# A mixture of experts in two groups of token tiles in place of three, and two small norm steps moved to GpSimd

## The reference, cut to what matters

```
t = _to_tokens(x)
t = t + _L0_ffn_ref(_ln_t(t), L0_ffn_Wg, L0_ffn_W1, L0_ffn_b1, L0_ffn_W2, L0_ffn_b2)
x = _from_tokens(t, x)
x = x + _L1_conv_ref(_ln_c(x), ...)
```

## Time and profile before

| | us |
|---|---|
| median of 3 runs | 867.4 |
| lowest and highest run | 866.68, 870.57 |
| the profiled execution | 865.79 |
| its span, first to last instruction | 864.0 |
| TensorE busy | 709.4 (82%) |
| VectorE busy | 559.6 (65%) |
| ScalarE busy | 353.9 (41%) |
| GpSimd busy | 276.7 (32%) |

### The profile page before, as it was taken

The page is one execution under the profiler, slowest core; times in us unless marked ns, Lnnn a source line. Parts: engine busy times, 40 slices in busy tenths (PEclk is TensorE's granted clock), DMA queues, the critical chain, the costliest instruction groups (busy, mean ns, idle before and its releaser), DMA issues.

```text
span 864.0 us, 13817 instructions
## 1 busy us (share of the span) xinstructions
PE 709.4 (82%) x4364; PEld 565.9 (66%) x4364; DVE 559.6 (65%) x2110; ACT 353.9 (41%) x889; POOL 276.7 (32%) x339
## 2 busy tenths in 40 slices
PE   6998988999779999979779985877875676686768
PEld 5886877988658999864368963555553443453336
DVE  7988742233342631477930225999999999989774
ACT  1000443554422223225412113887785664574322
POOL 5105162506440000024610022665555444533200
PEclk9999999999979999979979999999798999998989
DMA  8803255767500566600005100000000002001020
GB/s 345 295 1 98 79 163 149 205 184 217 214 14 26 195 219 241 246 1 0 1 1 201 56 1 0 1 2 1 2 1 1 1 4 47 2 13 50 13 50 25
DMA packets 27286, 72.64 MB, mean 84 GB/s; under 512 B 3000, under 2 KB 11576, under 8 KB 24528
## 3 DMA queue, kind: packets, MB, share of 16 engines
q1 hardware_dynamic: 25168, 67.56, 23.9%
q0 software_dynamic: 2048, 4.20, 1.6%
HBM read 61.61 MB, written 10.14 MB: 83 GB/s over the span
## 4 chain that ended last, share of the span: by engine, by line
PE 52%; DVE 31%; issue 6%; ACT 5%; POOL 5%; DMA 1%; SPq 0%; DVEq 0%; POOLq 0%; ACTq 0%
PE PB L1056 6%; PE PB L930 6%; PE PB L944 5%; PE PB L1272 5%; DVE arena L2633 3%; DVE top L2644 3%; PE PB L861 3%; DVE top L2628 3%; DVE arena L2647 3%; PE PB L851 2%; PE PB L1450 2%; DVE XT L1973 2%; PE PB L1034 2%; PE PB L1359 1%; PE PB L810 1%
## 5 line engine op out<-in xcount | busy, mean ns | idle before, releaser
L802 POOL TENSOR_TENSOR arena<-arena 128x512 f32<-128x512 f32 x64 | 81.3, 1270 | 120.9 <-ACT arena L1918 120.9
L1359 PE MATMUL PB<-ring 128*128 128x256 f32 x256 | 75.5, 422 | 17.7 <-ACT arena L1910 17.0
L1584 PE MATMUL PB<-w_first,arena 128*128 128x128 f32 x256 | 45.2, 304 | 52.6 <-POOL arena L802 52.0
L602 POOL TENSOR_TENSOR lnrs<-lnve,mhalf 128x4 f32<-128x4 f32 x20 | 20.5, 1026 | 210.1 <-DVE lnve L1956 206.0
L1634 ACT ACTIVATE arena<-PB,arena 128x128 f32<-128x128 f32 x212 | 60.2, 366 | 55.0 <-PE PB L930 55.0
L1584 PEld LDWEIGHTS PB<-w_first,arena 128*128 128x128 f32 x256 | 31.6, 153 | 77.7 <-POOL arena L802 72.7
L1918 ACT ACTIVATE arena<-arena,nmx 128x256 f32<-128x256 f32 x128 | 58.2, 506 | 58.8 <-DVE arena L2647 58.5
L930 PE MATMUL PB<-arena 128*128 128x128 f32 x424 | 60.2, 287 | 9.8 <-DVE arena L2172 5.3
L1359 PEld LDWEIGHTS PB<-ring 128*128 128x128 f32 x256 | 48.1, 209 | 29.6 <-issue 18.9
L930 PEld LDWEIGHTS PB<-arena 128*128 128x128 f32 x424 | 54.2, 201 | 12.9 <-issue 6.6
L944 PE MATMUL PB<-ring,arena 128*128 x424 | 59.5, 285 | 0.8 <-ACT arena L1634 0.7
(11 more groups left out here) (335 smaller groups left out, 1567.3 us busy)
## 6 DMA issues: line engine op xcount, KB each, us to landing
ring<-in_taps_dram SPq DMA_DIRECT2D x12, 1536.0 KB, 6.6
arena<-in_experts_dram SPq DMA_DIRECT2D x53, 258.0 KB, 3.3
ring<-in_taps_dram SPq DMA_DIRECT2D x7, 1792.0 KB, 7.4
arena<-comb_rows SPq DMA_DIRECT2D x6, 512.0 KB, 5.7
w_later<-in_later_dram SPq DMA_DIRECT2D x1, 2951.5 KB, 14.6
arena<-rows_there SPq DMA_DIRECT2D x11, 256.0 KB, 3.1
rows_back<-arena SPq DMA_DIRECT2D x11, 256.0 KB, 3.1
ring<-in_second_dram SPq DMA_DIRECT2D x1, 2048.0 KB, 18.4
```

The costliest lines, as they stand in the source:

```text
L802: g.tensor_tensor(PR[c % 2], E1[c % 2], E2[c % 2], ALU.subtract).then_inc(sub_ready, 1)
L1359: last = mm(PB[c % 2][:, q * 256:q * 256 + 256], QM[c // 2 % 3][:, o + P * q:o + P * q + P], Kc[:, N * s + HW * j:N * s + HW * j + HW], st ...
L1584: last = tr(PB[3][:, kt * 256 + q * P:kt * 256 + q * P + P], PR[c % 2][:, q * 256 + kt * P:q * 256 + kt * P + P], ident)
```

## The change

Groups are (0, 8) and (8, 8), so ROOM is 23 and 23, 46 uses in 12 chunks. Group 0 now holds slots 0 and 1, group 1 slots 2 and 3. Routing is still done in three steps (ROUTES): slot 0, slot 1, then slots 2 and 3 together. Slots 0 and 1 are both routed within the convolution's loop, with ranks(0) at its step 27 and place_rows(0) at step 26. Slots 2 and 3 are routed after the convolution and before the first use; place_rows(1) stands before the first turned_rows. GpSimd's two powers for slots 2 and 3 stand between the scatters of group 0. Gathers of slots 0 and 1 are paced by uses; gathers of slots 2 and 3 follow the last stored chunk, with a power between them.

```diff
-GROUPS = [(0, 4), (4, 8), (12, 4)]
+GROUPS = [(0, 8), (8, 8)]
-RANKS = [(5, 0), (7, P), (6, 0), (6, P)]
+RANKS = [(5, 0), (7, P)]
+ROUTES = [(0, 4), (4, 4), (8, 8)]
+ROUTE_OF = [0, 1, 2, 2]
...
 (part_pow, GpSimd)
                 pool.wait_ge(*at(ln_var[n], k + 1))
+                g.tensor_scalar(lnve[:, some], lnmv[:, some, 1], LN_EPS[n], None, ALU.add).then_inc(pow_done, 1)
+                g.tensor_scalar(lnst[:, some, 1], lnmv[:, some, 0], -1.0, None, ALU.mult).then_inc(pow_done, 1)
+                pool.wait_ge(pow_done, 3 * pows[0] + 2)
                 g.tensor_tensor(lnrs[:, some], lnve[:, some], mhalf[:, 0:m], ALU.pow).then_inc(pow_done, 1)
...
-                g.tensor_tensor(lnst[:, some, 0], lnmv[:, some, 0], lnrs[:, some], ALU.mult).then_inc(ln_rstd[n][0], 1)
+                g.tensor_tensor(lnst[:, some, 0], lnst[:, some, 1], lnrs[:, some], ALU.mult).then_inc(ln_rstd[n][0], 1)
...
 (GpSimd's program)
-            for t in range(0, 4):
+            for t in range(0, 8):
+                if t in (2, 4):
+                    ln_pow(1, 1 + t // 2)
                 scatter(t)
-            ln_pow(1, 2)
-            ln_pow(1, 3)
             pool.wait_ge(rows_placed, 2)
-            for t in range(4, 12):
+            for t in range(8, 16):
                 scatter(t)
-            pool.wait_ge(rows_placed, 3)
-            for t in range(12, 16):
-                scatter(t, 16 + 2 * (t - 12))
...
-            gather(0, 22)
+            gather(0, 25)
+            gather(1, 33)
             ln_pow(2, 0)
-            gather(1)
+            ln_pow(2, 1)
             gather(2)
-            ln_pow(2, 1)
+            gather(3, None, range(0, 2))
             ln_pow(2, 2)
-            gather(3)
+            gather(3, None, range(2, 4))
             ln_pow(2, 3)
...
 (TensorE, after the convolution's loop)
             ln_turn(1, 2, PB[6])
+            pe.wait_ge(router_shifted, 2)
             logits(0, 1, 2, W["Wg0"], PB[7])
             pe.wait_ge(x_after_conv, SLOTS)
+            ln_turn(1, 3, PB[6])
+            logits(0, 1, 3, W["Wg0"], PB[7])
+            ranks(1)
...
 (TensorE's loop over uses: removed)
-                if u == 3:
-                    ranks(1)
-                if u == 5:
-                    pe.wait_ge(*at(xn_ready[1], 3))
-                    ln_turn(1, 3, PB[6])
-                if u == 6:
-                    pe.wait_ge(rows_placed, 2)
-                    logits(0, 1, 3, W["Wg0"], PB[7])
-                if u == 10:
-                    pe.wait_ge(*at(xn_ready[1], SLOTS))
-                    ranks(2)
...
 (part_stats, VectorE)
-                after(k2)
-                some = slice(tiles[0], tiles[-1] + 1)
-                link(v.tensor_scalar(lnmv[:, some, 0], lnmv[:, some, 0], -1.0, None, ALU.mult))
-                v.tensor_scalar(lnve[:, some], lnmv[:, some, 1], LN_EPS[n], None, ALU.add).then_inc(ln_var[n][0], 1)
+                last.then_inc(ln_var[n][0], 1)
...
 (VectorE's convolution loop)
-                if c in (13, 21, 28):
+                if c in (13, 20, 28):
...
+                if c == 23:
+                    router_start(0, 1, slice(4, 8), PB[7])
+                if c == 24:
+                    pick_experts(1)
+                if c == 26:
                     place_rows(0)
...
 (VectorE, before and in the loop over chunks)
+            ln_apply(1, 3)
+            router_start(0, 2, slice(8, 16), PB[7])
+            pick_experts(2)
+            place_rows(1)
             turned_rows(0)
-            route_start(1)
-            turned_rows(1)
-            ln_apply(1, 3)
-            place_rows(1)
...
+                if q == 10:
+                    add_rows(1)
                 if q == 11:
-                    add_rows(1)
-                if q == 12:
                     ln_apply(2, 1)
-                    add_rows(2)
+            add_rows(2)
             ln_apply(2, 2)
             add_rows_by_tile(3)
```

More of the change, by code:

```diff
@@ L368, in metaformer @@
         combT_ready = S("combT_ready")
-        GROUPS_BEFORE = [0, NG, NG + 1]
+        GROUPS_BEFORE = [0, len(ROUTES), len(ROUTES) + 1]
         ffn_up_done = S("ffn_up_done")
@@ L378, in metaformer @@
         scattered = [S(f"scattered{g}") for g in range(NG)]
-        tile_gathered = [(scattered[g], 16 * 2 * GROUPS[g][1]) for g in range(NG)] + [(gathered[SLOTS - 1], 0)]
+        tile_gathered = [(scattered[g], 16 * 2 * GROUPS[g][1]) for g in range(NG)] \
+            + [(gathered[SLOTS - 1], 0), (S("gathered_last"), 0)]
         rows_landed = [(S("xg_in"), 0), (mods_in, 16), (later_in, 16)]
@@ L660, in scatter, with gather @@
                                          XT[:, t, :], None).then_inc(scattered[i], 16)
-            def gather(s, pace=None):
+            def gather(s, pace=None, tiles=range(TILES)):
                 i = GROUP_OF[TILES * s]
                 pool.wait_ge(y_stored, 16 * (FIRST_CHUNK[i] + len(GROUP_CHUNKS[i])))
-                for t in range(TILES * s, TILES * s + TILES):
+                for t in range(TILES * s + tiles.start, TILES * s + tiles.stop):
                     for k in range(2):
@@ L872, in ranks @@
                 pe.wait_ge(mods_in, 16)
-                pe.wait_ge(experts_picked, g + 1)
+                pe.wait_ge(experts_picked, g + 2)
                 m = picked2[:, E * (t0 + g):E * (t0 + g + n + 1)]
@@ L887, in _ @@
                     downsample(*todo.pop(0))
-                if c in (17, 24):
-                    s = c // 24
+                if c in (17, 23):
+                    s = c // 23
                     pe.wait_ge(x_in, SLOTS)
@@ L893, in _ @@
                     pe.wait_ge(later_in, 16)
-                if c == 25:
+                if c == 24:
                     pe.wait_ge(router_shifted, 1)
-                if c in (19, 25):
-                    logits(0, 1, c // 25, W["Wg0"], PB[7])
-                if c == 22:
+                if c in (19, 24):
+                    logits(0, 1, c // 24, W["Wg0"], PB[7])
+                if c == 27:
                     ranks(0)
@@ L979, in _ @@
                         pe.wait_ge(rows_placed, NG)
-                    comb_turn(0, GROUP_OF[TILES * s], s, PB[6])
+                    comb_turn(0, ROUTE_OF[s], s, PB[6])
                 if 0 <= s < SLOTS and u == CHUNKS[q][2]:
@@ L1614, in _ @@
             ln_copy(1, 1, PB[6])
+            router_act(0, 1, (1,))
             ln_copy(1, 2, PB[6])
-            router_act(0, 1, (1, 2))
+            ln_copy(1, 3, PB[6])
+            router_act(0, 2, (2, 3))
             def bias_weights(s):
@@ L1963, in part_stats @@
                     after(k - len(tiles) + 1 + i)
-                    k2 = mark(v.bn_aggr(lnmv[:, t, :], lnst[:, t, :]))
-                after(k2)
-                some = slice(tiles[0], tiles[-1] + 1)
-                link(v.tensor_scalar(lnmv[:, some, 0], lnmv[:, some, 0], -1.0, None, ALU.mult))
-                v.tensor_scalar(lnve[:, some], lnmv[:, some, 1], LN_EPS[n], None, ALU.add).then_inc(ln_var[n][0], 1)
+                    last = v.bn_aggr(lnmv[:, t, :], lnst[:, t, :])
+                last.then_inc(ln_var[n][0], 1)
             def ln_apply(n, s):
@@ L2020, in router_finish, with pick_experts @@
                 dve.wait_ge(comb_ready, group)
-            def pick_experts(g):
-                t0, n = GROUPS[g]
+            def pick_experts(i):
+                t0, n = ROUTES[i]
+                g = GROUP_OF[t0]
                 tiles = slice(t0, t0 + n)
@@ L2034, in pick_experts @@
                 v.memset(R(7), -2.0)
-                dve.wait_ge(router_exp, g + 1)
+                dve.wait_ge(router_exp, i + 1)
                 link(v.tensor_reduce(q(1), R(1), AX.X, ALU.add))
@@ L2054, in pick_experts @@
                 link(v.reciprocal(q(7), q(6)))
-                dve.wait_ge(experts_picked, g + 1)
+                dve.wait_ge(experts_picked, i + 1)
                 v.tensor_tensor(two, both, one, ALU.subtract)
@@ L2059, in pick_experts @@
                 v.tensor_tensor(comb[:, tiles, :], R(0), wide(q(7)), ALU.mult).then_inc(comb_ready, 1)
-                dve.wait_ge(comb_ready, g + 1)
+                dve.wait_ge(comb_ready, i + 1)
             def place_rows(g):
@@ L2146, in _ @@
                     ln_apply(0, 2 + c // 8)
-                if c in (13, 21, 28):
-                    finish(c // 7 - 2 if c > 13 else 0)
-                if c in (14, 22, 29):
-                    ln_apply(1, c // 7 - 2 if c > 14 else 0)
+                if c in (13, 20, 28):
+                    finish((13, 20, 28).index(c))
+                if c in (14, 21, 29):
+                    ln_apply(1, (14, 21, 29).index(c))
                 if c == 18:
@@ L2161, in _ @@
             dve.wait_ge(later_in, 16)
[L2162 to L2165, removed]
             def turned_rows(q):
```

14 lines of the change are left out of this document (3 added, 11 removed).

## The result

The changed kernel takes 879.66 us, median of four runs (878.68 to 881.14), against 868.99 for the kernel before in the same session: a ratio of 1.0131 (95% interval 1.0096 to 1.0167). It is slower by 10.7 us, and 879.66 lies above the range of 858 to 876. The profiled execution took 878.68, its span is 876.4 against 864.0.

A forecast was written before the change was run, and what follows sets the result against it. TensorE was taken to bound the steady expert loop, with a tail paced by GpSimd. Start and uses together -6.4, tail +9.5 and norms -3.5 sum to -0.4, so 867.0 us was predicted, range 858 to 876.

The forecast's parts named there:

- The start: Routing before the experts: the first use starts at about 116.4, against 90.10, 26.3 later.
- The end of 113.6: Early end for the first use's start, if TensorE is at full clock and logits don't keep VectorE waiting.
- The uses: Expert loop: 46 uses at 2.07, biases and start-up make 103.8 against 136.5; last copy at 220.2, 6.4 earlier.
- the upper end of its pace: Expert loop: a use costs 2.18 in place of 2.07, which adds 5.
- The tail: Last copy to line 1034: 16 gathers, not eight; 11.6 later, less 0.7 and 1.4 for the clock: 9.5 later.
- the 11.6: Tail: 10.2 for eight more gathers, 1.03 for slot 2's power and about 0.4 of waiting.
- the 0.7 that was only estimated: Tail: taken off because the last gathers no longer share DMA engines with the filter taps.
- The second rival: Tail: half clock after long idleness makes slot 2's products and set-up 11.9, line 1034 14.3 later; 873.5, chance 0.26.
- The norms: Late norms: VectorE loses two instructions 14 times, GpSimd does two steps more; 3.5 earlier in all.
- The first: Rival for the loop: TensorE runs uses at its own pace, 1.97; time 861.0, chance 0.32 with beyond.
- The tail's lower end: Tail: only 7.3 later, if all of the 2.8 lost to half clock comes back.
- the four terms: Start, uses, tail and late norms; their ends, added as independent, give about 9 to either side.

The follow-up runs named there:

- e8: Changed kernel plus products nobody reads in TensorE's waits, ahead of slot 3's turn, the counting, the first use and slot 2's tokens: 880.53 us.
- e1: Changed kernel with the first rows of group 1 (chunk 6) asked for at use 16 in place of use 20: 874.03 us.
- e5: Changed kernel with both loop repairs, rows of group 1 asked for earlier and six weight buffers in place of four: 863.94 us, ratio 0.9946 to the kernel before.
- e6: Kernel before (three groups) with the late norms' edit and six weight buffers: 860.75 us, ratio 0.9931.
- e2: Changed kernel with six buffers of expert weights in place of four: 872.0 us.
- e7b: Changed kernel with slot 2's rows fetched from group 0's store, ahead of slot 1's power on GpSimd (slot 2's output differs): 872.25 us.
- e3: Kernel before with the late norms' edit alone: 866.33 us, ratio 0.9953.
- e7: Changed kernel with slot 2's rows fetched from group 0's store, still behind slot 1's power on GpSimd (slot 2's output differs): 879.84 us.
- e11: Three groups with the norms' edit and six weight buffers, plus 23 unread products just ahead of the last slot's turn: 857.01 us, ratio 0.9839.

## Why the prediction was wrong, point by point

**The start: right.** Step by step it gave 116.4, and 116.97 was measured. The end of 113.6, "if TensorE is at full clock", was tried by e8, in part, since slot 3's turn stayed at 1.11: 115.37, with the load of rows the next thing late (TensorE waited 1.41 for it there).

**The uses: this step failed**, by 9.6 of the total miss of 10.1 at the end of line 1034's products (13.2 against -6.4 + 9.5 = 3.1): 113.4 measured, 103.8 forecast, and 108.8 with the upper end of its pace. Two of its sentences were wrong, and its sum had no term for loads of weights. "On SyncE's queue rows_in of group 1 then finds its rows long there": the rows were there, but a load begins when it is asked for, and the request stood behind weights that wait for a buffer. The row that should have warned is the wait of 3.79 at 133.50. The prediction let it go with "the waits for rows" of the old loop and did not ask what made them late. SyncE's timeline of the kernel before has the answer; ahead of it stands GpSimd's last scatter of that group:

```profile
124.12 0.96 POOL L659 DMA_INDIRECT rows_there<-XT,row_number  x1 [0.30 <-issue]
```

```profile
130.07 0.33 SPq L517 DMA_DIRECT2D arena<-in_experts_dram  x1
130.51 0.83 SPq L529 DMA_DIRECT2D arena<-rows_there  x2
```

The scatters had been issued by 125.1, and the load was asked for at 130.51, right behind a load of weights: the same order as in the changed kernel, where e1 removed the wait by the request alone. For the kernel before this is read from the order; no run tried it. And "I expect 46 x 2.07": e5 shows what a use costs with nothing late, 1.90. The 2.07 of the earlier trace rows held late weights already: with six buffers three groups take 1.90 too (e6, 7.58 for the chunk of four from 171.62). In the changed kernel loads were late more often than in the stretch of the earlier trace rows, and e2 shows this as 10.0 us. With both loads early enough the loop took 97.2, better than 103.8: the error was not in TensorE's work but in the assumption that SyncE keeps up. The prediction counted the power behind GpSimd's gathers, but on SyncE's queue only the rows, not the weights ahead of them.

**The tail: right**, term by term. 9.5 later predicted; 10.5 later at the line's start and 1.04 back in its products make 9.5. The last gather began 20.3 after the first, against 8.9 before: 11.4 of the 11.6. From there to the line it took 8.7, 0.9 less for the 0.7 that was only estimated, and the clock gave 1.0 for 1.4. That last one was luck: in e5 the products took 13.34, with nothing back. e7b shows that the mechanism is the eight gathers (9.9 sooner at the line without them). The second rival, half clock, decided by no more than 0.5: VectorE's last normalising (258.67, 1.11 long) was through at 259.8, and slot 3's turn began at 260.31, right behind the set-up at half clock (line 1022, 1.22 in place of 0.70). Slot 2's products and the set-up took 8.2, not that rival's 11.9, and the line began at 31.7 after the last copy, not at 35.5, although the granted clock over 240 to 260 was 0.63, below the 0.74 of before.

**The norms: mechanism right, size smaller.** 2.5 where they stand alone (e3; 2.0 by the profiles), not 3.5; GpSimd's steps took 0.28 and 0.23, as far as the rows of before allowed.

**The rivals.** The first needs loads that are never late: with e5's repairs the loop, 97.2, is even below its 99.2, and the time is 863.94, not 861.0; its full clock in line 1034 did not come (13.34). Its 1.97 was no pace either: the stretch of the earlier trace rows has two biases in it, which the sum adds once more. The second's time of 873.5 was nearer to the result than the forecast, but not by its mechanism. The other side, slower, came true through a mechanism that none of the three named: the queue that feeds the faster loop.

**Sums and readings.** The tail's lower end, "all of the 2.8 back", is 11.6 - 0.7 - 2.8 = 8.1, not 7.3. The ends of the four terms as independent give 9 upward but only some 6 downward. And in the slices of the first experts, 5 to 11 of the earlier trace rows, VectorE was busy for two to four tenths after the first of them, not "a third to two thirds". None of this moves the forecast.

## What to carry to other kernels

When a change lets an engine run faster, price each use's loads against the new pace: how far ahead each one is asked for, and what stands ahead of it on its queue; a pace read from a stretch in which loads were already late is not the engine's own. For a wait at the border of two groups, read the order of requests first; fewer borders did not remove it here. Fewer, larger groups make the loop shorter and both ends longer: here 33.1 less loop (e5's 97.2 against e6's 130.3, with late rows left in the second) were paid with 26.3 more start and 10.9 more tail.

## What the runs showed of the hardware

The granted clock fell to 0.71 for 9 us in which TensorE was busy without a gap (e8, 513 to 522), to 0.68 in the same work of e1's profile (511 to 520) and to 0.64 in e7's (511 to 520): 28 products took 9.10, 9.36 and 9.08 there, and 6.62 in the changed kernel, which kept 1.00, as the kernel before did. e1 and e7 have no unread products, and what brings the clock down there is open. Filling a wait did not always keep the clock. A gap of 2.72 behind the added work left slot 2's products at half clock (3.65, e8); with a gap of 0.65 the counting ran at full clock (1.90, e8), and with none the last line took 10.69 (e11). But in e8 ten unread instructions, 2.48 long and at half clock themselves, ran right up to slot 3's turn, and it took 1.11 all the same. Indirect gathers that ran beside two loads of 1536 KB took 6.8 to land, and 2.6 behind them (e7 and the changed kernel), so gathers issued 4.4 earlier brought their rows only 1.6 earlier.
